# Causal mask of the row maxima: from TensorE mask products to the VectorE instruction that takes the maximum

## The reference, cut to what matters

```
x = x + attn(layernorm(x))                      # x: (4, 2048, 256)
    qkv = x @ w_qkv ; Q, K = rope(Q), rope(K)   # 16 heads of 16
    s = (Q . K) * 0.25 ; s = where(causal, s, -1e9)
    out = softmax(s) @ V ; out @ w_proj + b_proj
x = x + ffn(layernorm(x))
    sqrt((x @ cos(theta + theta_noise))**2 + (x @ sin(phi + phi_noise))**2)
```

## Time and profile before

| | before |
|---|---|
| median of three runs | 2035.52 us |
| profiled execution, its own time | 2035.29 us |
| its span, first to last instruction | 2033.5 us |
| PE busy | 1998.3 us (98%) |
| DVE busy | 1508.7 us (74%) |
| ACT busy | 1390.4 us (68%) |
| POOL busy | 857.9 us (42%) |
| mean granted TensorE clock | 0.995 of full speed |

### The profile page before, as it was taken

One profiled execution on the slowest core, in us unless ns is written; L12 is line 12 of the kernel. 1 busy time (PEld: TensorE's weight loads), 2 busy tenths in 40 slices (PEclk: granted clock), 3 DMA queues, 4 the chain that ended last, 5 costly groups with the idle time before them and its releaser, 6 DMA issues.

```text
span 2033.5 us, 38813 instructions
## 1 busy us (share of the span) xinstructions
PE 1998.3 (98%) x13028; PEld 856.6 (42%) x13028; DVE 1508.7 (74%) x2757; ACT 1390.4 (68%) x2687; POOL 857.9 (42%) x1335
## 2 busy tenths in 40 slices
PE   7999999999999999999999999999999999999998
PEld 4343443344443444444444443444444344433334
DVE  5888787887778677786767868688677867667835
ACT  3367677776667676777667676687766767667774
POOL 3622425363443435543363442546434363351132
PEclk9999999999999999999999999999999999999999
DMA  6310222231111221221122111222111222130122
GB/s 140 74 43 17 69 61 70 62 84 55 57 60 55 68 70 58 75 87 61 60 65 73 63 55 53 80 87 73 58 54 60 70 70 79 29 117 6 48 89 68
DMA packets 130761, 133.35 MB, mean 66 GB/s; under 512 B 29435, under 2 KB 105723, under 8 KB 130555
## 3 DMA queue, kind: packets, MB, share of 16 engines
q1 hardware_dynamic: 127728, 128.29, 20.5%
q10 hardware_dynamic: 2832, 2.56, 0.7%
HBM read 38.49 MB, written 25.68 MB: 32 GB/s over the span
## 4 chain that ended last, share of the span: by engine, by line
PE 87%; POOL 3%; issue 2%; ACT 2%; DVE 2%; SPq 2%; DMA 1%; DVEq 0%; POOLq 0%; ACTq 0%
PE banks L1049 22%; PE banks L1064 22%; PE banks L1027 21%; PE banks L971 5%; PE banks L982 5%; PE banks L1025 3%; PE banks L1009 3%; PE banks L916 3%; DVE chunk_max L1361 2%; ACT probs L1168 1%; SPq L731 1%; PE banks L905 1%; PE banks L898 1%; POOL guess L664 1%; ACT inverse L1188 1%
## 5 line engine op out<-in xcount | busy, mean ns | idle before, releaser
L1361 DVE TENSOR_REDUCE chunk_max<-banks 128x1 f32<-128x512 f32 (+3 forms) x2240 | 1351.8, 667 | 404.8 <-PE banks L1027 401.9
L1168 ACT ACTIVATE probs<-banks 128x512 f32<-128x512 f32 (+1 forms) x2240 | 1139.2, 602 | 356.0 <-PE banks L1049 274.7
L1027 PE MATMUL banks<-stack_k,stack_q 96*128 96x512 bf16 (+3 forms) x2560 | 730.0, 349 | 1.8 <-DVE chunk_max L1361 0.7
L1049 PE MATMUL banks<-stack_q,stack_k 99*128 99x512 bf16 (+3 forms) x2560 | 694.6, 349 | 4.4 <-ACT probs L1168 2.2
L1064 PE MATMUL banks<-probs,v_one 128*17 128x512 f32 (+3 forms) x5120 | 528.5, 532 | 3.6 <-POOL probs L1488 2.8
L1049 PEld LDWEIGHTS banks<-stack_q,stack_k 99*128 99x128 bf16 x2560 | 229.3, 97 | 375.1 <-ACT probs L1168 182.2
L1027 PEld LDWEIGHTS banks<-stack_k,stack_q 96*128 96x128 bf16 x2560 | 240.3, 98 | 244.8 <-DVE chunk_max L1361 71.4
L1488 POOL TENSOR_SCALAR_AFFINE_SELECT probs<-probs 128x512 f32<-128x512 f32 x256 | 162.7, 644 | 350.9 <-ACT probs L1168 348.8
L1064 PEld LDWEIGHTS banks<-probs,v_one 128*17 128x17 f32 x5120 | 118.6, 96 | 280.3 <-issue 175.1
L1025 PE MATMUL banks<-diag_mask,ident_bf 128*128 128x128 bf16 x1024 | 199.2, 221 | 5.1 <-DVE chunk_max L1361 4.2
L1472 POOL TENSOR_SCALAR max_neg<-row_max 128x16 f32<-128x16 f32 x64 | 16.3, 255 | 313.5 <-DVE row_max L1370 239.4
(11 more groups left out here) (156 smaller groups left out, 1146.3 us busy)
## 6 DMA issues: line engine op xcount, KB each, us to landing
stack_q<-parts SPq DMA_DIRECT2D x384, 64.0 KB, 2.6
stack_k<-parts SPq DMA_DIRECT2D x354, 64.0 KB, 2.6
sums<-o_raw SPq DMA_DIRECT2D x64, 256.0 KB, 2.3
rot<-raw SPq DMA_DIRECT2D x236, 64.0 KB, 2.0
xin<-x SPq DMA_DIRECT2D x16, 512.0 KB, 4.1
heads_t<-sums SPq DMA_DIRECT2D x26, 256.0 KB
mid<-x SPq DMA_DIRECT2D x13, 512.0 KB, 4.1
inverse<-inverses SPq DMA_DIRECT2D x26, 256.0 KB
```

The source lines that it names most:

```text
L1027: mm = nc.tensor.matmul(bank[:, n * wide:(n + 1) * wide], stack_q[u % 2][0:SPLIT_ROWS, t, h + n, j * P:(j + 1) * P], stack_k[u % 2][0:SPLI ...
L1049: mm = nc.tensor.matmul(bank[:, a * wide:(a + 1) * wide], stack_k[u % 2][0:ROWS, j // SUB, first + a, (j % SUB) * P:(j % SUB + 1) * P], st ...
L1168: nc.scalar.activation(probs[:, g % PROBS, first:first + many, w0:SPAN], bank, ACT.Exp).then_inc(s_exp, 1)
L1361: nc.vector.tensor_reduce(to, bank[:, 0:count * wide].rearrange("p (h n) -> p h n", h=count), AX.X, ALU.max).then_inc(s_emptied["DVE"], 1)
```

## The change

Three edits.

1. In the diagonal chunk the mask products (L1025) are gone; the score products start the bank by themselves. VectorE masks and reduces in one instruction per head: `tensor_tensor_reduce` adds `row_mask` (bf16, zeros in the first 384 columns, the triangle in the last 128; the last `wide` columns are used) to the bank in place, in PSUM, and takes the maximum to `chunk_max`. `masks(count)` is true for every count up to four, so all 1024 head-tiles of the diagonal go this way. The 1 + 2 + 4 + 4 instructions of a pair become 16, and the build makes two engine instructions of each: the one that adds and reduces, and one that writes the result out.
2. The planner's durations follow: TensorE loses the 0.06 a head, VectorE gets 0.13 a head instead of 0.07 an instruction. The orders of all engines are planned anew.
3. Memory: `by_head` goes, and the denominators of all sets lie in the first 64 columns of `squares`; their load waits for the squares of the block before to be summed (and for the sines, the first time) instead of for the store of the previous inverses. `max_t` has one buffer, so that the copy of a pair waits for the DMAs of the pair before. POOL sets the zeros of `row_mask` in the beginning, one instruction more.

```
--- before.py
+++ after.py
 NEG = -1e30
+LOWEST = -3e38
...
+def masks(count):
+    return count <= MASKED_HEADS
 def max_width(tile, c):
+MASKED_HEADS = 4
 MAX_LEAD = 0.56
...
                 name, wide = ("max", u, tile, h, n, d), n * max_width(tile, d)
-                job(name, "PE", 0.01 + wide / 2400 + (0.06 * n if d == tile // SUB else 0.0), at + step * done / total - MAX_FIRST,
+                job(name, "PE", 0.01 + wide / 2400 + (0.06 * n if d == tile // SUB and not masks(n) else 0.0), at + step * done / total - MAX_FIRST,
                     [before_max, *((f, u, k) for f in ("fetch", "fetch_k") for k in range(c + 1)), begun(at + step * done / total - MAX_SLACK)])
-                with_bank(name, name, "DVE", 0.07 + wide / 970, at + step * done / total)
+                with_bank(name, name, "DVE", (0.13 if d == tile // SUB and masks(n) else 0.07 / n) * n + wide / 970, at + step * done / total)
                 before_max, done = name, done + wide
...
             stored = ("store", unit - (n == FINAL), t)
-            job(("den", n), "SP", 0.5, at, [stored, ("keepinv", prev), ("den", n - 1), begun(at - SLACK)], 2.2)
+            job(("den", n), "SP", 0.5, at, [stored, ("power", prev, 1), ("sin", KT - 1), ("den", n - 1), begun(at - SLACK)], 2.2)
             job(("heads", n), "SP", 1.1, at, [stored, ("wave", prev, SUB - 1), ("sin", KT - 1), ("heads", n - 1), *free], 2.5)
...
         ident_bf = sb("ident_bf", [P, P], BF16)
-        diag_mask = sb("diag_mask", [P, P], BF16)
+        row_mask = sb("row_mask", [P, SPAN], BF16)
+        diag_mask = row_mask[:, SPAN - P:SPAN]
         stack_q = [sb(f"stack_q{n}", [P, SPANS, HG, SPAN], BF16) for n in range(2)]
...
         max_parts = sb("max_parts", [P, 2, MAX_PARTS, HG * SUB], BF16)
-        max_t = sb("max_t", [MAX_PARTS * HG * SUB, 2, P], BF16)
+        max_t = sb("max_t", [MAX_PARTS * HG * SUB, P], BF16)
         stats = sb("stats", [P, SUB, 6])
...
         bias = sb("bias", [P, DIM])
-        by_head = sb("denominators", [P, 2, HEADS * SPAN // P])
         late = [x_t[:, :, :].rearrange("p k n -> p (k n)")]
...
         squares = [sb("squares", [P, 2, 2 * DIM])] + [t[:, 3, :].rearrange("p (j n) -> p j n", j=2) for t in late]
-        denominators = [by_head[:, 0, :], by_head[:, 1, :]] + [t[:, 0, 0:HEADS * SPAN // P] for t in squares[2:]]
+        denominators = [t[:, 0, 0:HEADS * SPAN // P] for t in squares]
         stats3 = sb("stats3", [P, SUB, 6])
...
             if n == 0:
-                engine.wait_ge(s_pool_setup, 5)
+                engine.wait_ge(s_pool_setup, 6)
             else:
...
                         sp.dma_start(to.rearrange("m h (j n) -> m (h j) n", j=SUB),
-                                     max_t[m * count:(m + 1) * count, i % 2, :]).then_inc(s_rows[i % 2], 16)
+                                     max_t[m * count:(m + 1) * count, :]).then_inc(s_rows[i % 2], 16)
...
                     sums_stored(n)
+                    if n == 0:
+                        sp.wait_ge(s_sin, KT)
                     if count:
-                        sp.wait_ge(s_keepinv[f], 16 * count)
+                        sp.wait_ge(s_power, 2 * prev + 2)
                     count = heads_by_memory(n)
...
                     for n in range(count):
-                        if c == t:
-                            nc.tensor.matmul(bank[:, (n + 1) * wide - P:(n + 1) * wide], ident_bf[:, :], diag_mask[:, :],
+                        if c == t and not masks(count):
+                            nc.tensor.matmul(bank[:, (n + 1) * wide - P:(n + 1) * wide], ident_bf[:, :], diag_mask,
                                              start=True, stop=False, skip_group_check=True)
                         mm = nc.tensor.matmul(bank[:, n * wide:(n + 1) * wide], stack_q[u % 2][0:SPLIT_ROWS, t, h + n, j * P:(j + 1) * P],
-                                              stack_k[u % 2][0:SPLIT_ROWS, c, h + n, 0:wide], start=c < t, stop=True, skip_group_check=True)
+                                              stack_k[u % 2][0:SPLIT_ROWS, c, h + n, 0:wide], start=c < t or masks(count), stop=True, skip_group_check=True)
                     mm.then_inc(s_filled["DVE"], 1)
...
                 fill(WARM)
-                pe.wait_ge(s_pool_setup, 5)
+                pe.wait_ge(s_pool_setup, 6)
                 for name in ORDER["PE"]:
...
                         i = TURN[u, t]
-                        if i >= 2:
-                            dve.wait_ge(s_rows[i % 2], 16 * MAX_PARTS * (i // 2))
-                        nc.vector.tensor_copy(max_t[:, i % 2, :], bank.bitcast(BF16)[0:MAX_PARTS * HG * SUB, 0:P]).then_inc(s_emptied["DVE"], 1)
+                        if i:
+                            dve.wait_ge(s_rows[(i - 1) % 2], 16 * MAX_PARTS * ((i - 1) // 2 + 1))
+                        nc.vector.tensor_copy(max_t[:, :], bank.bitcast(BF16)[0:MAX_PARTS * HG * SUB, 0:P]).then_inc(s_emptied["DVE"], 1)
                         return
...
                         dve.wait_ge(s_rowmax, i - 1)
+                    if c == tile // SUB and masks(count):
+                        dve.wait_ge(s_pool_setup, 6)
+                        for n in range(count):
+                            scores_of = bank[:, n * wide:(n + 1) * wide]
+                            ins = nc.vector.tensor_tensor_reduce(out=scores_of, in0=scores_of, in1=row_mask[:, SPAN - wide:SPAN], scale=1.0, scalar=LOWEST,
+                                                                 op0=ALU.add, op1=ALU.max, accum_out=chunk_max[:, i % 2, tile % SUB, h + n:h + n + 1, c])
+                        ins.then_inc(s_emptied["DVE"], 1)
+                        return
                     to = chunk_max[:, i % 2, tile % SUB, h:h + count, c]
...
                 nc.gpsimd.memset(power_t[:, :], -0.5).then_inc(s_pool_setup, 1)
+                nc.gpsimd.memset(row_mask[:, 0:SPAN - P], 0.0).then_inc(s_pool_setup, 1)
                 pool.wait_ge(s_ident, 16)
                 pool.wait_ge(s_corner, 16)
-                nc.gpsimd.tensor_copy(diag_mask[:, :], corner_t).then_inc(s_pool_setup, 1)
+                nc.gpsimd.tensor_copy(diag_mask, corner_t).then_inc(s_pool_setup, 1)
                 for name in ORDER["POOL"]:
                         deviation(pool, nc.gpsimd, name[1])
```

## The result

The changed kernel takes 2019.58 us (median of five runs, 2015.97 to 2024.51) against 2035.82 us: 0.9924 of before, 95% interval 0.9906 to 0.9942. It is faster, as forecast, but by 16 us, where the forecast was 35 (2001 us; the likeliest case reached from 1986 to 2015, the whole range from 1980 to 2034).

The account below looks back on a forecast made before the run. The prediction took TensorE to bound the kernel except at the start and very end. 2035.3 - 61.4 (products) + 12.8 (order) + 3 (stalls) + 5.2 + 3.5 (start) + 2.5 (end) = 2000.9, said as 2001 us; range 1980 to 2034, likeliest 1986 to 2015.

Parts of the forecast that it names:

- What bounds the kernel: Whole span: TensorE, 98% busy, sets the time, except the first 150 us (VectorE has a part) and the very end.
- 87% of VectorE alone does not delay TensorE: Later 50 us stretches: VectorE busy 43.7 and 43.3 us goes with TensorE busy 50.0 and 49.9, so no delay.
- 3 us for stalls: From 150 to 1750 us: allowance for VectorE stalls where a short pair's maxima make mask work thick, 3 us.
- the start (5.2 + 3.5) and the end (2.5): First 150 us: removed products give nothing (5.2), half of VectorE's extra shows (3.5); behind 1750 us half the saving lost (2.5).
- The products, 1024 x 0.06 = 61.4 us: TensorE, diagonal chunk: 1024 mask products go, each holding the next product back about 0.06 us, 61.4 us removed.
- The order, +12.8 us: TensorE: 361 instead of 303 groups of value products, 58 more changeovers at 0.22 us each, 12.8 us added.
- VectorE, 81 us more: VectorE, diagonal maxima: 5 more instructions and 16 write-outs a pair at 0.06 us each, over 64 pairs, 81 us.
- rival C: VectorE: masked maximum takes twice 1.05 ns a column, 425 us more work, kernel slower at 2155 us; chance 0.13.
- rival B: VectorE: write-out waits for its partner, 0.27 us each, 296 us in all, giving 2027 us (2015 to 2035); chance 0.14.
- The other edits: Single max_t buffer, POOL's added memset, denominators' load and bank use: claimed to cost nothing.
- Rival D: Some mishap of max_t or denominators, or a copy stalling 0.5 us a pair behind its DMAs, some 2033 us; chance 0.03.
- rival A: Removal shows nearly whole: start bound by TensorE's order, changeovers partly fall into waits, 1980 us; chance 0.13.

Follow-up runs that it names:

- e5: Changed kernel in the old order (planner's durations of before), VectorE taking plain maxima over unmasked diagonal squares, no mask products: 2012.6 us, 0.9893 of the kernel before.
- e1: Changed kernel planned with the durations of before, so all engines keep the old order; masked maxima kept, no mask products: 2035.7 us, 1.0005 of the kernel before.
- e10: Changed kernel with VectorE's plain maxima reading only half of their columns, masked maxima in full: 2008.1 us, 0.9869 of the kernel before.
- e11: Changed kernel with ScalarE's exponentials of full banks computing only half of their columns from the 41st step on: 2003.9 us, 0.9858 of the kernel before.
- e13: Changed kernel with both VectorE's plain maxima and, from the 41st step, ScalarE's full-bank exponentials halved in columns: 1980.7 us, 0.9737 of the kernel before.
- e2: Kernel before with all its instructions, mask products included, but planned with the new durations (new order, 361 groups): 2056.0 us, 1.0106 of the kernel before.
- e3: Changed kernel in its new order, but VectorE takes plain maxima over unmasked diagonal squares: 2015.7 us, 0.9910 of the kernel before.
- e7: Changed kernel planned with near-measured masked-maximum durations and holding each kind of product longer (RUN 4.0, STICK 0.1; 278 groups): 2025.3 us, 0.9956 of the kernel before.
- e4: Kernel before with the memory edits alone (MASKED_HEADS = 0), mask products, old maxima and old order of first scores: 2034.9 us, 1.0000 of the kernel before.

## Why the prediction was wrong

The direction was right and the size was not: 16 us instead of 35. By its own steps:

- **"What bounds the kernel": this step failed.** "So the span is TensorE's work" was read off a busy share of 98% and a few microseconds of idle time. Removing 61.4 us of that work in the old order gives 22 us with VectorE's old instruction (e5) and none with the new (e1). From 150 to 1750 us, which the prediction gave to TensorE whole, e5 gains 18.9 us for 51.2 removed. Between the groups of value products TensorE fills one bank for VectorE and one for ScalarE in 0.44 us; VectorE takes 0.60 us for its bank, ScalarE 0.48. The time of a removed mask product is mostly spent waiting for a bank instead. The 99.5% did not show this, because a late start hides under the record of the product in front.
- **"87% of VectorE alone does not delay TensorE" failed with it.** The average of 50 us says nothing about 3 us between two groups. e10, e11 and e13 show that these two engines pace the changed kernel in part: with each a quarter less busy, the same TensorE program takes 1980.7 us. The same was not run on the kernel before, nor with more banks, which could let TensorE run ahead at the same paces; so how much lies in the engines' paces and how much in the few banks is open. My 3 us for stalls from 150 to 1750 us was the term that stood for this; with the start (5.2 + 3.5) and the end (2.5) the sum gave back 14.2 of the 61.4 us. In the new order 21 are given back by the removal itself (e2 to e3, -40), about 4 by the heavier maximum: 25 instead of 14.2. These 11 us and the 8 that the order costs beyond its term are the 19 by which the forecast was off.
- **The products, 1024 x 0.06 = 61.4 us.** Number and size were right as work (61.0 us from start to start). The page counts 12,012 products instead of 13,028: 1024 fewer mask products and 8 more identity products as fillers (L1082, 76 instead of 68), which the new plan puts in. As time the mask products were worth 19 to 40 us.
- **The order, +12.8 us.** 21 (e2). The way it was counted, changeovers times 0.22 us, does not carry over to other orders: e7 has fewer and is slower. From start to start e2's value products take 10.4 us more than before and its first scores 8.1. What the 8 us beyond the changeovers are was not told apart; waits and stretches of lower clock are both in e2's trace (mean clock 0.993, before 0.995).
- **The clock, which had no term.** The five timed runs of the changed kernel had 0.990 to 0.996 of full clock; the one with 0.996 took 2015.97 us, 3.6 us below the median. The kernel before ran at 0.994 to 0.997 beside the experiments. So about 4 of the missing 19 us go with the lower clock, inside the terms above and not beside them.
- **VectorE, 81 us more.** 58 us in the records. The bound at the lower end, 0.06 us for the write-out, was too high: the pair holds the engine 0.01 us longer than a plain maximum at 384 and 512 columns, and has 0.05 us more of fixed part at 128. The main instruction runs at about the maximum's pace a column; rival C's doubling and rival B's wait for the partner do not occur. B's 2027 is nearer to the measured time than the forecast's 2001, and its range of 2015 to 2035 holds it, but by luck: its mechanism is not there. What this work costs depends on the order: some 4 us or less in one that was planned for it, 21 to 23 in one that was not. I had priced it as 3 + 3.5.
- **The other edits, nothing.** Right (e4: 2034.9 us).
- **Rival D** fell with e4, **rival A** (1980) with the change itself.
- Of the signs I had named, TensorE's busy share above 98% came true (1584.25 of 1600 is 99%) and proved nothing, and of the sign for B and C, a VectorE over 90% busy there and weight loads that wait tens of microseconds for the masked line, the second half came true (39.9 us) beside a VectorE at 80% (1277.02 of 1600), with neither B nor C right. Both signs were too blunt for the question.

## What to carry to other kernels

Where an order was planned against several engines at once, a busy share of 98% on one does not make its work the span: list the waits of its weight loads over the whole run, since a late start under the record of the product in front shows nowhere else, and compare the pace at which it hands out banks with the pace of those that empty them, stretch by stretch. What an instruction is worth can then be bounded only from its neighbours' slack; here the same 61 us were worth 0 (together with a heavier partner), 19, 22 or 40. Before believing a removal, run the old order without the removed work: it needs only the planner's old durations and separates the order from the instructions.

## What the hardware showed that I had not expected

- The write-out of a reduction's result has a record of 0.14 us and takes next to no time: the next instruction mostly starts with it (51.08 and 51.08 above), and the pair of main instruction and write-out is only 0.01 us longer than the plain maximum at 384 and 512 columns. At 128 and 256 columns its fixed part is 0.05 us larger than the plain one's; whether that is the write-out's or the main instruction's is not told apart. An addition with a maximum that reads PSUM and bf16 SBUF and writes PSUM runs at 0.93 ns a column from 128 to 512 columns ((0.607 - 0.248) / 384), and the plain maximum at 1.04 from 384 to 512 ((0.598 - 0.465) / 128). This agrees with what the Trainium skill, "VectorE: DVE Perf Modes", section "Two Vector instructions with no wait between them", says of such pairs, that the second is an instruction of its own and held only under conditions; what it costs, the page does not say.
- TensorE's clock fell to its lower level in the middle of the changed kernel's profiled execution, where it had not before (1.00 from 150 to 1750 us). From 1300 to 1350 us TensorE was busy for 48.48 of the 50 us, with a mean granted clock of 0.93; the finer rows show a stretch of 7 us at 1.2 GHz, and just before it a TensorE that was busy for only 1.04 of 2 us:

```profile
1300.00:1350.00 50.00, 48.48 (x261) 16.24 (x260) 39.23 (x122) 37.84 (x71) 22.56 (x44) 0.93 0.25 81
...
1324.00:1326.00 2.00, 1.04 (x5) 0.19 (x2) 1.75 (x3) 1.97 (x3) 1.73 (x2) 1.00 0.00 0
...
1327.00:1334.00 7.00, 7.00 (x29) 2.28 (x27) 5.05 (x22) 4.53 (x11) 5.19 (x10) 0.51 0.39 114
```

A shorter one, at 317 us, came behind two waits of TensorE for GpSimd of 0.80 and 1.73 us.

The five timed runs of the changed kernel spread over 8.5 us (before: 3.0), and their mean clock goes with it: 0.996 for 2015.97 us, 0.994 for 2018.04, 0.992 for 2019.58, 0.991 for 2022.42, 0.990 for 2024.51. That the waits bring the lower clock about was not tested; that the runs with more of it are the longer ones is what the numbers show.
